# One block instead of two: the second attention's first stages move into the last steps of the first, its second batch and the weights' rounding to later units

## The reference

```
x = x + cross_attention(norm(x), ctx)       # 16 heads of 64, 4096 keys, biases
x = x + self_attention(norm(x))             # 16 heads of 16, 256 keys
        q = xn @ W_q ; latent = (xn @ W_k + xn @ W_v) @ W_down_kv      # 64 wide
        k = latent @ W_up_k ; v = latent @ W_up_v
        scores = (q k^T / 16) * exp(-0.01 |i-j|) ; softmax ; @ v ; @ W_o
x = x + ffn(norm(x))                        # 704 wide: silu(gate) * up, then down
        each operand of the three FFN products, weights too, is first rounded to
        FP4 in blocks of 16 (scale = max|.|/6, values 0 .5 1 1.5 2 3 4 6)
```

## Time and profile before

| | |
|---|---|
| median of 3 runs | 1324.57 us (1323.09 to 1327.39) |
| the profiled execution, its own time | 1324.31 us |
| its span in the trace | 1322.6 us |
| PE busy | 1277.8 us (97%), POOL 947.9 (72%), DVE 881.7 (67%), ACT 881.7 (67%) |
| last step of cross attention ends | 1149.9 us from the span's start |
| scores of unit 0, of unit 2 | 1178.12, 1180.33 us |
| values of the last unit end | 1271.03 us |

### The profile page before, as it was taken

The page is one execution under the profiler, slowest core; times in us unless marked ns, Lnnn a source line. Parts: engine busy times, 40 slices in busy tenths (PEclk is TensorE's granted clock), DMA queues, the critical chain, the costliest instruction groups (busy, mean ns, idle before and its releaser), DMA issues. The chain is left out here.

```text
span 1322.6 us, 25021 instructions
## 1 busy us (share of the span) xinstructions
PE 1277.8 (97%) x9210; PEld 1107.2 (84%) x9210; DVE 881.7 (67%) x1408; ACT 881.7 (67%) x1721; POOL 947.9 (72%) x1096
## 2 busy tenths in 40 slices
PE   5899999999999999999999999999999999798998
PEld 5788888888888888888888888888888888567875
DVE  3666667666766677667666676667666766748557
ACT  3677776667767666777676776666777667548641
POOL 4877897789867976788778977898779777117310
PEclk9999999999999999999999999999999999989989
DMA  4010000000001001110000000000000001200000
GB/s 135 18 41 13 17 1 9 9 17 1 9 9 33 1 17 41 41 49 1 17 1 17 1 9 10 17 1 9 9 1 1 1 9 33 72 1 1 1 1 16
DMA packets 24904, 22.97 MB, mean 17 GB/s; under 512 B 4432, under 2 KB 24528, under 8 KB 24784
## 3 DMA queue, kind: packets, MB, share of 16 engines
q1 hardware_dynamic: 24784, 21.38, 5.3%
HBM read 20.85 MB, written 0.52 MB: 16 GB/s over the span
## 5 line engine op out<-in xcount | busy, mean ns | idle before, releaser
L684 ACT ACTIVATE pT_hi<-psT 128x512 fp32r<-128x512 f32 x512 | 293.4, 601 | 242.9 <-PE psT L437 239.6
L774 DVE TENSOR_TENSOR pT_lo<-psT,pT_hi 128x512 fp32r<-128x512 f32 x512 | 330.1, 685 | 103.1 <-ACT pT_hi L684 102.4
L768 DVE TENSOR_REDUCE negm<-psS 128x1 f32<-128x1024 f32 x256 | 311.4, 1217 | 20.5 <-PE psS L427 16.9
L336 POOL TENSOR_TENSOR kT<-kraw,khi 64x512 fp32r<-64x512 f32 x252 | 324.0, 1286 | 0.0
L647 ACT ACTIVATE prob<-psS,negm 128x1024 f32<-128x1024 f32 x256 | 285.5, 1115 | 1.0 <-DVE negm L768 1.0
L437 PEld LDWEIGHTS psT<-ident,prob 128*128 128x128 f32 x2048 | 230.2, 141 | 65.2 <-issue 36.8
L437 PE MATMUL psT<-ident,prob 128*128 128x128 f32 x2048 | 273.5, 276 | 3.8 <-DVE pT_lo L774 3.8
L453 PE MATMUL psO<-pT_hi,v 128*128 128x256 f32 x1024 | 268.7, 295 | 2.9 <-DVE pT_lo L774 1.2
L454 PE MATMUL psO<-pT_lo,v 128*128 128x256 f32 x1024 | 256.8, 282 | 0.0
L453 PEld LDWEIGHTS psO<-pT_hi,v 128*128 128x128 f32 x1024 | 194.7, 190 | 5.3 <-DVE pT_lo L774 2.9
L427 PE MATMUL psS<-kT,q_hi 64*128 64x512 f32 x1024 | 194.8, 416 | 3.4 <-ACT prob L647 2.0
(11 more groups left out here) (258 smaller groups left out, 1669.1 us busy)
## 6 DMA issues: line engine op xcount, KB each, us to landing
cst<-in_ctx_dram SPq DMA_DIRECT2D x12, 512.0 KB, 3.9
wraw<-in_L_xattn_Wk_dram SPq DMA_DIRECT2D x8, 256.0 KB, 2.7
wraw<-in_L_xattn_Wv_dram SPq DMA_DIRECT2D x8, 256.0 KB, 2.7
wraw<-in_L_xattn_Wq_dram SPq DMA_DIRECT2D x8, 256.0 KB, 2.6
wo<-in_L_xattn_Wo_dram SPq DMA_DIRECT2D x8, 256.0 KB, 2.7
oT<-in_ctx_dram SPq DMA_DIRECT2D x2, 512.0 KB, 5.5
prob<-in_ctx_dram SPq DMA_DIRECT2D x2, 512.0 KB, 4.7
ff_wdn<-in_L_ffn_w_down_dram SPq DMA_DIRECT2D x1, 704.0 KB, 7.5
```

The costliest lines, as they stand in the source:

```text
L336: pool.tensor_tensor(kT[half, m // 2 % KRING, h, 1, :], raw[own, :], khi[own, :].bitcast(F32), ALU.subtract).then_inc(k_split, 1)
L684: act.activation(pT_hi[:, i % PRING, :], psT[:, t % 2, :], ACT.Copy).then_inc(ph_ok, 1)
L768: dve.tensor_reduce(negm[:, g % 2, h, qt, c:c + 1], psS[:, qt, :], AX.X, ALU.max, negate=True)\
L774: dve.tensor_tensor(pT_lo[:, i % PRING, :], psT[:, t % 2, :], pT_hi[:, i % PRING, :].bitcast(F32), ALU.subtract).then_inc(pl_ok, 1)
```

## The change

Both functions become one, `perceiver_layer`, with one block. The tiles of the later layers that are needed early lie in the room of the context, the others over the cross attention's tiles, in the same bytes as tiles that are dead by then.

- Normalization, turning and the projections x, latent, q, k, v are done per batch. Batch 0's run inside the steps N-4 to N-1 through `psW`, the decay table one step earlier, and the scores of units 0 and 1 inside step N-1. Its statistics are taken in steps N-12 and N-11 and its root by GpSimd (`newton`, 14 small instructions, then two normalizing ones) ahead of the splits of step N-7.
- Batch 1's projections run in units 11 to 15. Its statistics are taken in units 8 and 9, its root and normalization by GpSimd between the operations 4 and 7 of chunk 1.
- The last group's merges 2 and 3 move into units 2 and 3, `turn_o` to unit 5, `project_o` to unit 6, `add_y` to unit 7. Both sums of these merges move from VectorE to GpSimd, ahead of the chunks.
- `WEIGHT_AT` and `TURN_AT` lie three units later. Each unit up to 28 masks q for its own batch only (256 columns instead of 512).
- The `idle` products of the seam and of units 2 and 3 go; one comes in each of the last three rounds of the loop, four ahead of `turn_xq(1)`, two ahead of `turn_h(3)`. `hidden(1)` comes ahead of `normalize(1)`, `residual(3)` ahead of `turn_h(3)`.

```
-    WEIGHT_AT = {0: (0, 1, 3), 1: (2, 4, 6), 2: (5, 7, 9), 3: (8, 10, 12), 4: (11, 13, 15), 5: (14, 16, 18)}
-    TURN_AT = (7, 10, 13, 16, 19, 22)
+    WEIGHT_AT = {0: (3, 4, 6), 1: (5, 7, 9), 2: (8, 10, 12), 3: (11, 13, 15), 4: (14, 16, 18), 5: (17, 19, 21)}
+    TURN_AT = (10, 13, 16, 19, 22, 25)
...
+        PROJECT_AT = {11: "x", 12: "lat", 13: "q", 14: "k", 15: "v"}
...  GpSimd
+                if n == N - 7:
+                    input_norm(0)
                 split_piece(n + LEAD)
                 split_v(n + LEAD)
...
+            for k in range(2, 4):
+                add_out(GP - 1, k)
+            for c in range(CHUNKS):
...
+                pool.wait_ge(wq, wq_at[c, 3])
+                pool.tensor_tensor(blocks(a), blocks(src), wide(wrs), ALU.mult).then_inc(wp, 1)
+                if c == 1:
+                    input_norm(1)
+                pool.wait_ge(wq, wq_at[c, 6])
...  TensorE, last steps of cross attention
+                elif n == N - 4:
+                    turn_x(0, psW[:, :])
+                elif n == N - 3:
+                    combine_kv()
+                elif n == N - 2:
+                    pe.wait_ge(proj_ok, projected(0, "q"))
                     post(g, 0, psW[:, :])
+                elif n == N - 1:
+                    pe.wait_ge(proj_ok, projected(0, "k"))
+                    unit_v(0, psW[:, :])
...
+                elif n == N - 3:
+                    project_lat(0, psW[:, :])
...
+                elif n == N - 1:
+                    unit_scores(0)
...
+                elif n == N - 4:
+                    turn_kv()
+                elif n == N - 3:
+                    pe.wait_ge(proj_ok, projected(0, "lat"))
+                    unit_q(0, psW[:, :])
+                elif n == N - 2:
+                    wait(pe, comb, 8 * g + 2 * 1 + 1)
+                    unit_k(0, psW[:, :])
+                elif n == N - 1:
+                    unit_scores(1)
...  TensorE, the units
+            for i in range(2, U + 3):
+                if i < U:
+                    unit_scores(i)
+                if i == LATE:
+                    pe.wait_ge(proj_ok, projected(0, "v"))
+                    post(GP - 1, 2, psW[:, :])
+                if i == LATE + 1:
+                    post(GP - 1, 3, bank_S[0])
+                if i == LATE + 3:
+                    turn_o(GP - 1)
+                if i == LATE + 4:
+                    project_o(GP - 1)
+                if i < U + 2:
+                    unit_turn(i - 2)
+                if turns_at(i) is not None:
+                    turn_w(turns_at(i))
+                if i in PROJECT_AT:
+                    kind = PROJECT_AT[i]
+                    same_bank_free(kind, 1)
+                    project[kind](1, saP[:, bank_of(kind, 1), :])
...
+                if i >= U:
+                    pe.wait_ge(wt_ok, NG)
+                    idle(saP[:, 0, 0:D], 1)
+                if i >= 3:
+                    unit_values(i - 3)
...
+            pe.wait_ge(eg_ok, 2)
+            idle(saT[:, 0, 0, :], 4)
+            turn_xq(1)
...  VectorE
+                if u >= 1:
+                    unit_max(u)
+                if u in (LATE, LATE + 1):
+                    weigh_out(GP - 1, u - LATE + 2, psW[:, :] if u == LATE else bank_S[0])
                 for c, op in weight_ops(u):
                     weight_op(c, op)
+                if u == LATE + 5:
+                    add_y(GP - 1)
+                if u in (LATE + 6, LATE + 7):
+                    input_statistics(QT + u - LATE - 6)
+                if u == LATE + 7:
+                    input_guess(1)
...
+            hidden(1)
             normalize(1)
             dve.wait_ge(fxn_ok, 4)
             round_chain(CHAIN_X, input_rows(1), range(10))
-            hidden(1)
```

More of the change, by code:

```diff
@@ new lines, in _, with same_bank_free, turn_kv @@
+            project = {"x": turn_x, "lat": project_lat, "q": unit_q, "k": unit_k, "v": unit_v}
+            def same_bank_free(kind, which):
+                old = two_visits_ago(kind, which)
+                if old is not None and old[0] == "w":
+                    pe.wait_ge(wt_ok, old[1] + 1)
+                elif old is not None:
+                    pe.wait_ge(proj_ok, projected(1, old[0]))
+            def turn_kv():
+                pe.wait_ge(proj_ok, projected(0, "x"))
+                pe.wait_ge(tail.kv_ok, 1)
+                for half in range(KT):
+                    for kt in range(KT):
+                        last = pe.transpose(psW[:, half * D + kt * P:half * D + (kt + 1) * P],
+                                            tail.w[:, 0, kt, half * P:(half + 1) * P], ident[:, :])
+                last.then_inc(tail.kvT_ps, 1)
@@ new lines, in turn_xq @@
+            def turn_xq(half):
+                if half == 0:
+                    pe.wait_ge(first_p, 4)
+                else:
+                    pe.wait_ge(chain, chain_end(CHAIN_X))
+                for kt in range(KT):
+                    for j in range(2):
+                        r = 2 * half + j
+                        last = pe.transpose(saO[:, half, kt, j * P:(j + 1) * P], xnf[:, r, kt * P:(kt + 1) * P],
+                                            ident[:, :])
+                last.then_inc(xt_ps, 1)
@@ new lines, in residual, with down @@
+            def residual(r):
+                pe.wait_ge(x1_ok, r // 2 + 1)
+                pe.wait_ge(xt_ok, r % 2 + 1)
+                if r >= 2:
+                    pe.wait_ge(res_ok, r - 1)
+                mm(psD[:, r % 2, 0, :], ident[:, :], y[:, r, :], start=True, stop=False)
+            def down(r):
+                for half in range(2):
+                    if r == R - 1 and half == 1:
+                        pe.wait_ge(hT_more, 1)
+                    else:
+                        pe.wait_ge(hT_ok, 2 * r + half + 1)
+                    for j in range(FH * half, FH * half + FH):
+                        last = mm(psD[:, r % 2, 0, :], hT[0:rows_of(j), r % 2, j, :], wdT[0:rows_of(j), j, :],
+                                  start=False, stop=(j == FT - 1))
+                last.then_inc(d_ps, 1)
@@ L641, in _ @@
+            down(1)
+            turn_h(2)
+            down(2)
+            residual(3)
+            pe.wait_ge(eg_ok, R)
+            idle(saT[:, 0, 0, :], 2)
+            turn_h(3)
+            down(3)
         @block.scalar
```

1349 lines of the change are left out of this document (652 added, 697 removed).

## The result

The changed kernel takes 1309.25 us in the median of four runs (1306.82 to 1315.80), the kernel before 1324.40 in the same session; the ratio is 0.9892, with a 95% interval of 0.9857 to 0.9927. Six more runs in another session gave 1308.68 (1306.60 to 1317.32) and 0.9898 [0.9874, 0.9922]. So it is faster, as predicted, by 15 us in place of 23.5, and just inside the upper end of the range by the median and outside it by the ratio (0.9892 x 1324.57 = 1310.3).

A forecast was written before the change was run, and what follows sets the result against it. Bounds: the seam's chain of small pieces, GpSimd with VectorE in rounding units, TensorE in later units. 20.5 us gained by chunk 5, then -1.3 + 0.3 + 2.1 + 1.9, gave 23.5: 1300.8, median 1301, range 1292 to 1310.

The forecast's parts named there:

- The seam: Last cross attention step to unit 2's scores: 30.4 us removed, 5.1 added to steps N-4 to N-1, unit 2 at 1155.0.
- so nothing: First norm on GpSimd at step N-7: delays the splits by 3.3 us but costs nothing, with 0.6 us to spare.
- the 8.4 of a chunk and 0.9: Chunk 0's operation 6 to chunk 1's: a chunk's 8.4 us plus 0.9 for `project_o` and `add_y`, ending at 1178.9.
- So I count the 6.1 in full: Second norm between GpSimd's operations 4 and 7 of chunk 1: a 6.1 us stall, less 0.3 for VectorE answering faster.
- two normalizing instructions, each between 0.3 and 0.72; I take 0.5: GpSimd's larger norm instructions, in no row: priced at 0.5 us each, between a 256-column sum and a 512-column cast.
- I count them at nothing: Batch 1's five projections: 4.8 us of TensorE hidden in the stall and in units paced by GpSimd; 3 without that cover.
- The rest: From unit 21 on: -1.3 for turns and last chunk, +0.3 idle products, +2.1 gate 0, +1.9 through gate 2 and `hidden(2)`.
- as the profiled execution: Whole kernel: 1300.8 from the profiled execution's 1324.31, the median of the runs 0.26 us above it, so 1301.
- The smaller stall: Rival at units 9 to 11: GpSimd has slack before unit 11, the 5.8 us go, time 1295; chance 0.18.
- The fallen clock: Rival at unit 11 and chunk 1's turn: the stall lowers the clock, about 5 us more, 1307 with projections uncovered; chance 0.20.
- what the profile will show: Signs; wrong if N-4 to N-1 stretch over 8 us, units 9-12 take 2.8 each, or clock under 0.9 from 1155 to 1250.
- the 1302: Units 3 and 4: GpSimd's merge sums could stop VectorE through the shared port pair, up to 1.2 us more, time 1302.

The follow-up runs named there:

- kv_less: Kernel `all` with half of batch 1's k and v products left out, so its output is another: 1302.60 us.
- short_root: Changed kernel with one root iteration in place of three for batch 1's norm, so its output is slightly another: 1305.47 us.
- norm_act: Changed kernel with batch 1's two normalizing instructions on ScalarE in place of GpSimd: 1305.87 us.
- stats7: Kernel `all` with both of batch 1's statistics in unit 7 and the guess of its root in unit 8: 1304.37 us.
- no_idle: Changed kernel without the idle products of the last three units, ahead of batch 1's second turn and ahead of the last turn of hidden: 1313.83 us.
- again: The changed kernel run once more, unaltered, for its spread and a second profile: 1308.68 us.
- norm0_early: Changed kernel with batch 0's norm on GpSimd in step N-9, two steps earlier: 1306.52 us.
- norm_dve: Changed kernel with batch 1's two normalizing instructions on VectorE in unit 10 in place of GpSimd: 1312.74 us.
- half_sums: Changed kernel without the second half of each sum in batch 1's latent and q projections, so its output is another: 1308.94 us.
- q_first: Changed kernel with batch 1's q projected in unit 12, ahead of the latent in unit 13: 1306.98 us.
- sums_dve: Changed kernel with both sums of the last merge on VectorE again, behind each weighing in units 2 and 3: 1313.55 us.
- all: Changed kernel with `norm_act`, `norm0_early`, `q_first` and idle products in units 3, 8, 9, 11, 17 and 18: 1305.31 us, ratio 0.9855.
- warm_only: Changed kernel with only more idle products, in units 3, 8, 9, 11, 17 and 18, none behind a late wait: 1307.52 us.

## Why the prediction was off by six microseconds

**The seam: right in the sum, in part by luck.** 5.1 us had been added to the steps; unit 2 starts 0.24 earlier than predicted, less than its start moves between executions. From the last value products of one step to those of the next, the steps N-4 to N-1 grew by 2.0, 1.8, 0.3 and 0.8 us, where 0.9, 2.7, 0.3 and 1.2 were predicted. Step N-4 was over its price since the first norm made W_k + W_v late, and the turn of it waited 1.68 us ("so nothing" was the prediction's price for that norm); step N-3 was under it by nearly as much.

**Chunk 0: right** within 0.6 (operation 6 ends at 1168.97; 1169.6 predicted).

**Chunk 1, the step that I took from too few rows:** 9.3 us were predicted from chunk 0 to chunk 1, as "the 8.4 of a chunk and 0.9". The kernel before had taken 10.28 there, in rows that the prediction did not use, and it is 10.87 now, with a statistic and `add_y` more. In both kernels VectorE waits 1.9 us for the scores of the unit behind chunk 0's operation 6, and the negation that follows is held to 1.0 or 1.1 us. 1.6 us lost.

**"So I count the 6.1 in full": right in kind, mis-sized by 1.7.** The wait ahead of unit 11's operation 0, forecast at some 5 us, is there with 6.47. The term of "two normalizing instructions, each between 0.3 and 0.72; I take 0.5" measured 1.23 each. The bound itself was wrong: an instruction with two scalars per row is not between a sum and a cast. The same error stands in the first norm.

**"I count them at nothing" (the projections of batch 1): the step that failed in kind.** It says that they lie in the stall and in units that GpSimd paces. For x, latent and q that was so. For k and v it was not: TensorE is busy without a pause from 1190 to 1206, unit 16's scores stand at the end of a chain of TensorE alone that begins at 1196.20, VectorE waits 1.41 us for them (0.64 in the kernel before), and 3 to 4 takes 10.06 in place of 8.21. Of the 1.85 between them 0.78 is that the maximum comes later behind operation 6 (1.98 us in place of 1.20). The other 1.07 is VectorE's unbroken run from this maximum to chunk 4's operation 6, 8.08 us in place of 7.01: the negation in it starts behind the start of GpSimd's operation 8, where it had ended ahead of it before, and takes 1.59 in place of 0.48. The prediction had read this hold-up at L1569, but had not asked which other small instructions would fall into it once TensorE is late. `kv_less` gives most of it back with half of k and v. TensorE also shows in 2 to 3, which is 8.4 behind the long stall at full clock, and 9.05 to 10.23 behind the shorter stalls with all of k and v (8.61 with half of them). That is why a cut of the stall pays only in part: 1.35 of 2.3 us in `short_root`, 1.3 of 2.2 in `norm_act`; in `stats7`, where the earlier statistics also cost VectorE 1.06, 0.2 of 2.4. The 3 us that the prediction had as the price of lost cover were a fair bound.

**From chunk 4 to 5** 0.75 were lost against the kernel before, 0.9 against the 8.4 that I had used for each chunk. VectorE has two things more in that stretch, in which it does not wait from 1215.11 to 1222.81: batch 0's weighing in unit 19 (0.29 + 0.76), and the negation of 1.67 us in place of 0.17, which starts 0.03 us behind GpSimd's operation 8 where it started 0.08 ahead of it before. Against both stands a wait of 1.53 us for scores that only the kernel before had there. No run took either out, so how they share the loss is argued, not shown.

**The rest** was 3.0 gained by prediction and is 2.4 (85.03 us from the maximum of unit 21 to the end before, 82.65 after). The gates came out as said: 4.68 to 2.61 and 4.30 to 2.60, and `no_idle` shows why. By stretches, the one up to gate 0 is 1.25 longer (1.0 predicted), the one to gate 2 is 2.0 shorter (2.1), the last one 1.6 shorter (1.9).

So, against the prediction's own numbers: 0.6 won up to chunk 0, then 1.6 (0 to 1), 1.65 (1 to 2), 1.65 (3 to 4), 0.9 (4 to 5) and 0.6 (the rest) lost, together 5.8 of the 6.0 us between 1300.8 and the 1306.82 of the profiled execution. The median of the runs is 2.4 above that execution, and there the step "as the profiled execution" failed: lapses of the clock cost 0 to 10 us, by where they fall.

**The rivals.** The smaller stall did not come: operation 7 waited by the list's order, as I had held against it. The fallen clock did come (0.50 from 1180 to 1185, 0.82 to 1190), but mostly in a stretch in which TensorE had a wait for the norm ahead, so in this execution it cost little; in `again` it fell later and 2 to 3 took 1.3 more. By the sign in "what the profile will show", a clock under 0.9 anywhere between 1155 and 1250, the prediction was to be wrong, and the profile has one (0.50 and 0.82). The sums of the last merge did not stop VectorE: beside GpSimd's at 1158.51 and 1160.74 its instructions have their usual lengths (0.42, 0.17 and 0.94 us), so the 1302 that the prediction worked out by the Trainium skill, "SBUF — State Buffer", Who interferes with whom, does not come from them, and on VectorE the sums cost 0.7 more.

## What to carry to other kernels

Work that is moved into a stall is hidden only as long as the stall is; look at how full the other engine is in the units right behind it, since whatever shortens the stall then pays only in part. A small VectorE instruction that starts just behind a long GpSimd one can take its length: ask not only how late an engine gets, but on which side of such an instruction the next one falls. Take the distance that you want to change from the rows of that very place, not from the average of its neighbours. A kernel whose clock lapses at changing places has a median above its best runs: a few idle products in the pauses that precede the lapses buy the spread, if they wait for nothing themselves. The best version here, both norms moved and with idle products, takes 1305.3 us, 3.4 under the changed kernel. The 1304.1 with the statistics earlier are mostly not the edit's, as said.

## What the runs showed of the hardware that I had not expected

- On GpSimd a subtract-and-multiply with two scalars per row takes 1.23 us for 128x256 fp32 (2.45 for two), where a sum of the same size takes 0.72. ScalarE took 1.09 for two, VectorE 0.90 alone and 3.87 beside GpSimd's 1.80 us instructions.
- VectorE's 128x2 negation takes 0.17 us. Started 0.24 us behind a GpSimd instruction of 1.81 us it took 1.59, started 0.03 behind one of 1.67 it took 1.67, each time until that one's end. Started 0.19 (`kv_less`) or 0.08 us (before) ahead of one it took 0.17. TensorE being 0.1 us later can so cost 1.5 us of VectorE.
- The granted clock fell in every profile of the changed kernel and of its variants without more idle products, to 0.50 or 0.52 for 5 us or longer in most, to 0.73 to 0.79 over 5 us in `again` and `norm0_early`. It fell behind pauses of TensorE (0.98 and 1.22 us ahead of the lapse at 1180 in the changed kernel), but at different places of the same code: around 1163 (`norm_dve`, `half_sums`, `no_idle`), 1183 (after, `q_first`, `short_root`), 1193 and 1223 (`sums_dve`). With twenty idle products in those pauses all runs of `all` had a mean of 0.997, those of `warm_only` 0.996 or 0.997. The Trainium skill, "TensorE: Matmul & The Clock Gate", What's actually happening, says that low is the default and activity releases the clock, and that in the first products of a kernel the moment of the change varies from run to run. The traces agree with the first, and show such a variation in the middle of a kernel too.
- A pause of 1.34 us at 1160 was followed by a lapse in some executions and by none in others, with the same instructions in the same order.
